# Attention: the turn of a step's maxima moved behind the first three query-major units of the next step

## The reference, cut to what matters

```python
scores = einsum('bnhd,bmd->bhnm', q, k) / sqrt(D)   # causal: keys m <= n alone
attn = softmax(scores, axis=-1)
out = einsum('bhnm,bmd->bnhd', attn, v)
```

## Time and profile before

| | before |
|---|---|
| three runs | 1034.52, 1038.93, 1037.01 us; median 1037.01 |
| the profiled execution | 1033.92 us, span 1032.2 us |
| PE, DVE, ACT, POOL busy, share of the span | 94%, 73%, 56%, 40% |
| mean granted TensorE clock | 0.984 of full speed |
| steady attention steps | from about 125 to 266 us and from 634 to 773 us |

### The profile page before, as it was taken

One profiled execution on the slowest core, in us unless ns is written; L12 is line 12 of the kernel. 1 busy time (PEld: TensorE's weight loads), 2 busy tenths in 40 slices (PEclk: granted clock), 3 DMA queues, 4 the chain that ended last, 5 costly groups with the idle time before them and its releaser, 6 DMA issues.

```text
span 1032.2 us, 19370 instructions
## 1 busy us (share of the span) xinstructions
PE 969.5 (94%) x6562; PEld 625.6 (61%) x6562; DVE 750.2 (73%) x1820; ACT 573.1 (56%) x1078; POOL 409.4 (40%) x434
## 2 busy tenths in 40 slices
PE   4888999999889999999999899999999899999997
PEld 3433333333348889988886433443334588899887
DVE  6788888888346686447868988888882668754475
ACT  4525767777753335653445657777777533466432
POOL 3420635322534507716653202323225361374570
PEclk9969999999999999999999999999999999999999
DMA  4720222110205315644239524333401251266351
GB/s 142 189 50 10 66 44 45 42 41 13 48 9 172 125 46 156 187 114 129 82 93 217 137 41 71 64 64 77 75 14 44 84 174 51 82 192 158 118 183 48
DMA packets 66754, 95.40 MB, mean 92 GB/s; under 512 B 19669, under 2 KB 50821, under 8 KB 64599
## 3 DMA queue, kind: packets, MB, share of 16 engines
q1 hardware_dynamic: 46645, 52.74, 18.9%
q10 hardware_dynamic: 13100, 22.53, 8.7%
q0 software_dynamic: 6912, 18.88, 7.2%
HBM read 66.79 MB, written 26.67 MB: 91 GB/s over the span
## 4 chain that ended last, share of the span: by engine, by line
PE 72%; DVE 13%; DMA 4%; issue 3%; ACT 3%; POOL 2%; SPq 1%; ACTq 0%; DVEq 0%; POOLq 0%
PE o_ps L1092 13%; PE st_ps L1075 10%; PE su_ps L1034 8%; PE st_ps L284 7%; PE st_ps L285 6%; PE st_ps L286 6%; PE st_ps L1034 4%; PE o_ps L1232 3%; PE su_ps L1138 3%; PE su_ps L1232 3%; DVE mab L1716 2%; PE st_ps L1267 2%; DVE unread L1714 2%; DVE xn L1595 1%; PE su_ps L284 1%
## 5 line engine op out<-in xcount | busy, mean ns | idle before, releaser
L1437 ACT ACTIVATE pt<-st_ps 128x512 f32<-128x512 f32 (+1 forms) x584 | 314.7, 596 | 159.5 <-PE st_ps L1075 150.8
L1075 PE MATMUL st_ps<-qs,ks 99*128 99x512 bf16 (+9 forms) x768 | 212.5, 329 | 5.4 <-DMA qs<-nmx 3.3
L798 POOL TENSOR_SCALAR_AFFINE_SELECT pt<-pt 128x512 f32<-128x512 f32 x120 | 74.4, 637 | 315.3 <-ACT pt L1437 315.3
L1034 PE MATMUL su_ps<-ks,qs 102*128 102x512 bf16 (+7 forms) x538 | 160.0, 330 | 7.5 <-DVE mc L1716 2.8
L1092 PE MATMUL o_ps<-pt,vp 128*32 128x512 f32 (+3 forms) x1536 | 155.5, 502 | 0.0
L1716 DVE TENSOR_REDUCE mab<-su_ps 128x1 f32<-128x512 f32 (+2 forms) x211 | 137.6, 684 | 13.0 <-PE su_ps L1034 12.2
L1034 PEld LDWEIGHTS su_ps<-ks,qs 96*128 96x128 bf16 (+1 forms) x538 | 51.7, 98 | 109.2 <-DVE mab L1716 45.5
L879 POOL DMA_INDIRECT rows_in<-rows,source x80 | 78.6, 983 | 98.0 <-DVE source L1975 73.7
L1075 PEld LDWEIGHTS st_ps<-qs,ks 99*128 99x128 bf16 (+2 forms) x768 | 73.4, 99 | 65.3 <-ACT pt L1437 16.9
L1714 DVE CUSTOM_DVE_ANT_0 unread<-su_ps,cst 128x384 f32<-128x384 f32 (+1 forms) x168 | 99.4, 612 | 17.8 <-PE su_ps L1034 17.7
L1463 ACT CAST hh<-hf 128x512 fp32r<-128x512 f32 x64 | 39.7, 621 | 123.9 <-DVE hf L1930 121.7
(11 more groups left out here) (234 smaller groups left out, 2061.3 us busy)
## 6 DMA issues: line engine op xcount, KB each, us to landing
wu_raw<-w_units_dram SPq DMA_DIRECT2D x32, 384.0 KB, 3.2
outs<-rows_out ACTq DMA_DIRECT2D x40, 256.0 KB, 3.2
q_parts<-hml SPq DMA_DIRECT2D x16, 384.0 KB, 3.3
wexp_raw<-w_units_dram SPq DMA_DIRECT2D x16, 384.0 KB, 6.7
inv<-inverses SPq DMA_DIRECT2D x128, 32.0 KB, 1.8
rows<-xn SPq DMA_DIRECT2D x8, 512.0 KB, 6.0
qs<-q_parts ACTq DMA_DIRECT2D x10, 384.0 KB
k_parts<-hml SPq DMA_DIRECT2D x8, 384.0 KB, 2.9
```

What stands on the lines that cost most here:

```text
L798: pool.affine_select(block, block, [[0, 4], [1, P]], ALU.is_ge, 0.0, base=0, channel_multiplier=-1).then_inc(masked, 1)
L1034: last = pe.matmul(out_b[:, c0:c0 + width], query_columns(s, slice(0, rows), j0 + a, P * qt, P * qt + P), key_stack(l, s)(j0 + a)[0:rows, ...
L1075: last = pe.matmul(out_b[:, at:at + hi - lo], key_stack(l, s)(j)[0:rows, P * kt:P * kt + P], query_columns(s, slice(0, rows), j, lo, hi), ...
L1437: act.activation(exponentials(S, q)[:, j, 0:width_of(s, q)], bank[KM_BANKS[i % len(KM_BANKS)]][:, 0:width_of(s, q)], ACT.Exp, scale=1 / np ...
```

## The change

`unit_number` gives the turn of steps 2 to 6 the place in the rotation of banks behind units 0, 1 and 2 of the step after, and those units the numbers before it. In PE's order this turn comes behind unit 2 of the next step; in VectorE's the join stays directly behind unit 37, and the four parts come ahead of unit 3 of the next step. The turns of steps 1 and 7 stay directly behind unit 37. `lead` goes from 0.2 to 0.28, and the reciprocals come ahead of units 9 and 30 in place of 6 and 27.

```diff
+def turned_late(s):
+    return 2 <= s < STEPS - 1
+
+def unit_number(S, u):
+    s = S % STEPS
+    if u == NSU - 1 and turned_late(s):
+        return unit_base(S) + u + UNITS_AHEAD
+    if u < UNITS_AHEAD and turned_late(s - 1):
+        return unit_base(S) + u - 1
+    return unit_base(S) + u
+
+UNITS_AHEAD = 3
...
+    passed = np.cumsum(np.insert(cost[:-1], UNITS_AHEAD, cost[-1])) / cost.sum()
+    passed = np.append(np.delete(passed, UNITS_AHEAD), 1.0)
...
     for s in range(2, STEPS):
-        for u, t in enumerate(s - 1 - lead + through):
+        for u in range(NSU):
+            t = s - 1 - lead + (passed[u] if turned_late(s - 1) else through[u])
             while at[n] < t - 1e-9 or u > 1 and n < FIRST_PIECES - 1:
                 n += 1
-            behind[n].append((s, u))
+            if u < NSU - 1 or not turned_late(s):
+                behind[n].append((s, u))
+            if u == UNITS_AHEAD - 1 and turned_late(s - 1):
+                behind[n].append((s - 1, NSU - 1))
...
-UNITS_BEHIND = [units_behind_pieces(l, 0.2) for l in range(2)]
+UNITS_BEHIND = [units_behind_pieces(l, 0.28) for l in range(2)]
...
-INVERT_AT, DIVIDE_BEHIND = (6, 27), (2, 4)
+INVERT_AT, DIVIDE_BEHIND = (9, 30), (2, 4)
...
+            def join_maxima(l, s):
+                S = step_no(l, s)
+                a = S % 2
+                dve.wait_ge(su_used, unit_base(S) + NSU - 1)
+                dve.tensor_tensor(mc[:, a, :, HALF:QT], mab[:, a, 0, :, :], mab[:, a, 1, :, :], ALU.max).then_inc(mc_done, 1)
...
             def maxima_parts(l, s):
-                n = unit_base(S) + NSU - 1
+                n = unit_number(S, NSU - 1)
                 a = S % 2
-                dve.wait_ge(su_used, n)
-                dve.tensor_tensor(mc[:, a, :, HALF:QT], mab[:, a, 0, :, :], mab[:, a, 1, :, :], ALU.max).then_inc(mc_done, 1)
                 dve.wait_ge(su_ready, n + 1)
...
+                            if u == UNITS_AHEAD and turned_late(s):
+                                maxima_parts(l, s)
                             maximum(l, s + 1, u)
-                        maxima_parts(l, s + 1)
+                        join_maxima(l, s + 1)
+                        if not turned_late(s + 1):
+                            maxima_parts(l, s + 1)
```

More of the change, by code:

```diff
@@ L176, in added_before @@
     if at >= 0:
-        return unit_base(S) + ADDED[at] + 1
-    return unit_base(S - 1) + ADDED[at] + 1 if S else 0
+        return unit_number(S, ADDED[at]) + 1
+    return unit_number(S - 1, ADDED[at]) + 1 if S else 0
 def units_behind_pieces(l, lead):
@@ L1015, in query_major @@
                 qt, half, j0, share, width, _ = SU[u]
-                n = unit_base(step_no(l, s)) + u
+                n = unit_number(step_no(l, s), u)
                 if s and u == 0:
@@ L1702, in maximum @@
                 S = step_no(l, s)
-                n = unit_base(S) + u
+                n = unit_number(S, u)
                 dve.wait_ge(su_ready, n + 1)
```

## The result

The changed kernel takes **1059.88 us** (median of 4 runs, 1059.72 to 1061.7) against 1036.09 us of the kernel before in the same set (4 runs, 1034.52 to 1038.93): a ratio of **1.0229 [1.0212, 1.0246]**. It is slower by 24 us where 13 were forecast, and above the range of 1039 to 1056. The profiled execution has a span of 1058.0 us against 1032.2, 25.8 more, at a mean granted clock of 0.976 against 0.984. Run again beside the second group of experiments it gave 1060.54 us, 1.0223 [1.0197, 1.0250].

The account below looks back on a forecast made before the run. The prediction took attention to be bound by PE's queue, run nearly without a gap. Steps 3 to 6 (+3.8), into step 2 (+1.5) and into step 7 (+1.2) made 6.5 us a layer, +13: 1050 us named, range 1039 to 1056.

Parts of the forecast that it names:

- The parts behind three maxima, and what they meet: VectorE's four parts queue behind three maxima, then GpSimd's products hold them; next first piece 8.4 or 9.5 us, not 7.33.
- The first rival, no hold: GpSimd's products don't stop VectorE's parts, or VectorE gets its turn between them: +4 us, 1041; chance 0.18.
- The faster case: Maxima come in time and PE keeps the gains at the turn, unit 36 and banks: 1029 to 1032 us; chance 0.08.
- the absorbed one: Each step starts later, but PE catches up within the same step: within 3 us of before; chance 0.10.
- the slack: How much later the maxima's DMAs could be issued without delaying the next step's first piece: 0.9 us.
- The recovery of 0.7 a step: PE saves unit 36's issue (0.21), its stall (0.24) and smaller bank waits (0.25 us) within each step.
- Unit 36's two terms: On PE, unit 36's issue of 0.21 us and its stall of 0.24 for a free bank are saved.
- smaller bank waits elsewhere: VectorE starts a step with nothing left over, so PE's other bank waits shrink by 0.25 us, an estimate.
- The step of the two kinds: Steps 3 to 6: +0.4 us where one GpSimd product follows, +1.5 where two follow, two steps of each a layer.
- Into step 2: Eleven units, not eight, behind step 0's last piece (+0.9 us) and a later first piece (+0.6): +1.5 a layer.
- Into step 7: Turn not late but stalls 1.6 us; maxima's DMAs go out 1.9 later, less 0.7 recovered: +1.2 us a layer.
- The upper bound of +20: Whole kernel: every last part held by a second product, and the 0.25 us not recovered ten times: +20 us.

Follow-up runs that it names:

- the kernel kept busy: The changed kernel with six matmuls of 512 columns, later overwritten, run on PE ahead of the first piece's wait in steps 3 and 5: 1090.99 us, 1.0161 of before.

## Why the prediction was right or wrong

The direction and the mechanism of the late parts were right; the size was half of it, because three terms of the sum were wrong or missing.

*The parts behind three maxima, and what they meet* was right to a tenth. The first part was to start 1.91 behind the join and starts 1.89 behind it (214.52 to 216.41); the cast was to be held to 0.5 and takes 0.48; the last part was to take up to 1.5 where a second product follows and takes 1.39, and 0.28 elsewhere; the first piece was to come 3.2 behind the first issue, and with a landing of 1.9 it does. Making the products wait removed both holds (0.21 and 0.28). That a product would hold as a memset and a select did was my estimate from the earlier trace rows; the runs show it: the cast and the last part end 0.07 and 0.14 behind a product's end, and the last part takes 0.28 with GpSimd quiet (608.65). By what mechanism, no run shows. The first rival, no hold, is refuted. Its one piece of evidence, the cast at 211.12 that took 0.21 beside a select, had come too late in the select to show a hold, 0.09 ahead of its end at 211.21: with the lead of 0.32 the cast at 187.23 took 0.33 and ended 0.08 behind its select.

*The faster case and the absorbed one* fell with the slack. Two units fewer would have done: with one ahead, the wait is gone. That would still not have been the faster case, since the turn then stands for 0.88.

*The recovery of 0.7 a step* failed in the part that was an estimate. Unit 36's two terms (0.21 and 0.24) are found at unit 36; the 0.25 of "smaller bank waits elsewhere" is not, and unit 36's 0.24 comes back at other units. Counted from starts, the even step that ends with the turn at 215.44 has, against the one of before that ends at 210.18: bank waits of 0.48 in place of 0.50, the turn's stall 0.45 in place of 0.52, 0.26 ahead of piece 33, where PE waits for an exponential and before did not, and 0.54 at the first piece. That is +0.71 of the +0.73. The step of the two kinds costs +0.73 and +1.81 in place of +0.4 and +1.5, at full clock and with a landing of 1.9. The cleanest measure is the kernel whose products wait: by my terms it should have had 27.94 - 0.7 + 0.73 (its first piece at V+8.06 in place of 7.33) = 27.97 and has 28.40. The last term is off by 0.4 there: about 0.3 a step over the eight late steps, 2.6 us in all.

*A term the sum did not have: the clock.* I asked what PE waits for, and not what PE does after it has waited. From a first piece to the next join it takes 22.18 us at full clock (162.21 to 184.39 in the changed kernel run again, and the same in steps 3 and 5 of the kernel kept busy), and in after 23.54 behind 162.31, 23.54 behind 223.36 and 23.69 behind 743.42: +1.36, +1.36 and +1.5, 4.2 us. That this goes with PE standing is what all twelve traces say together; that it comes of it is inferred. In steps 3 to 6 the clock fell eleven times, each time within 1.5 us of the end of a wait of 1.45 us or more, and never in the kernels without such waits. Behind the waits of 2.7 to 3.2 us in step 5 it fell in seven of eight, and behind the two that were filled with matmuls it did not. Behind waits of 1.45 it fell in two of seven, so in these steps such a wait lay ahead of every fall, but not every such wait had one behind it, and what decides is not known. In step 1 of the second layer it fell with no late first piece ahead (the windows from 620).

A further 2.05 us stands at a low clock behind the second layer's attention. Before has such a stretch there too, a shorter one (3.4 us against 6.9). Nothing was run that ties its length to the change, and it is as short as in before, 3.4 us, in two kernels that keep the late turns (ends as before, reciprocals back); it stays open.

*A second such term: the landing.* In step 5 the third of the maxima's DMAs lands in 3.1 us (first layer) and 3.4 (second), where most take 1.8 to 1.9 (see below), and the wait is 2.71 and 3.00 in place of some 1.45. That is +1.25 and +1.55. In both cases the DMA view shows one packet of the instruction queue, 16 KB, at that time (the line is of the window 221 to 224), and none around step 3 of the first layer:

```profile
q8 instruction: 1, 0.02, 2.0%
```

No run was made to try this, but the twelve traces bear it out. Of the 360 DMAs of the maxima of steps 2 to 6, 20 have such a packet starting within 1.5 us behind their issue, and they land in 2.3 to 3.7 us; 24 have it 1.5 to 1.9 us behind, and land in 1.8 to 2.0; the 293 with no packet of 8 KB or more beside them land in 1.8 to 1.9. In before the packet of step 5 comes at 216.2, when the maxima have landed; in after they go out 2.4 us later behind the join and meet it. Before has a landing of 3.6 us of this kind in step 2 of the first layer, and there the first piece (132.28) does wait for it, 0.98 us. The sum did not use that row (before, the maxima's tile in the window 126.5 to 130), which could have told of the term:

```profile
DMA to landing us min/median/max: 1.8/2.0/3.6
```

*The ends.* Into step 2, +3.0 was said for both layers: steps 1 and 2 together have +0.74 and +3.83. Step 1 varies by 0.9 us between the two traces of the changed kernel (27.21 and 28.09, first layer). The +1.5 of step 1 in the second layer goes with its low clock. It is not tied to the longer burst: that period is 26.1 us in three kernels that have the burst and no such stretch, and 29.8 in the one with the old burst and a stretch. Into step 7, +1.2 a layer was said, and +0.6 and +1.3 found. Giving the ends their old lead gained some 2 us in the median.

The account of the 25.8 us: 13 as forecast; the failed recovery, +2.6; the clock in steps 3 and 5, +4.2; the landings, +2.8; steps 1 and 2, +1.6 (about the low clock in step 1 of the second layer); step 7, -0.5; behind the second attention, +2.05. Sum 25.75.

The failed step, then, is the sum over steps 3 to 6: +3.8 a layer was said, +9.1 and +8.2 were measured. It took every landing as 1.9 where step 5 had 3.1 and 3.4 (2.8 us), priced each wait at its own length and the clock behind it at nothing (4.2 us), and allowed 0.25 a step of recovered bank waits that are not there, beside a turn's stall mis-sized by 0.07 (2.6 us). The upper bound of +20 fell with it, since it was made by adding holds alone.

## What to carry to other kernels

A result moved behind other work is late by everything that its instructions then queue behind, on each engine: here two maxima of 0.61 us used up a slack of 0.9, and the neighbour's two products of 1.3 held what came after. Count that slack first; if it goes, price the wait by its length and by the clock behind it (here 1.36 to 1.5 us where it fell). And to give a consumer distance from its producer, put work between them that makes nothing for the producer's engine: two pieces and a row of values ahead of the turn took its stall away, three units did not.

## What the runs showed of the hardware

- PE's granted clock fell from 1.00 to 0.50 behind single waits in a queue otherwise full: behind 1.46, 2.71 and 3.00 us of standing in after, and 1.77 in the kernel with a lead of 0.32. It did not fall behind 1.45 in after (second layer) and in its second run, nor behind 2.69 in step 2 of the kernel that fills only steps 3 and 5, nor behind 3.16 in the one with the old ends. With the reciprocals back it fell behind a wait of 1.45 (162.25). Length alone does not say which. In after it was back at 1.00 4.5 and 4.9 us behind the end of the wait (windows from 162 and from 223), and 3.7 behind that of 3.00.
- Such a stretch costs 1.35 to 1.5 us of the step, where the windows from 162 to 168 have PE at the lower level for some 3.4 us (twice the missing 0.15, 0.50 and 0.20, times 2 us). Half of that, 1.7, is an estimate of what the lower clock takes; where the rest of it went was not traced.
- With six matmuls that compute nothing in such waits the clock did not fall behind them, and the kernel was not slower but faster: 1.0161 [1.0129, 1.0194] against 1.0229 [1.0212, 1.0246] and 1.0223 [1.0197, 1.0250], measured in different sets.
- A 0.28 us VectorE instruction took 1.39 beside a GpSimd product, a 0.21 one 0.48, while what reads the score banks (st_ps, su_ps) beside the same first product kept its time: the reduction at 215.81 with 0.68, the two parts at 216.41 and 216.71 with 0.27 and 0.28.
- A DMA of 8 KB of the maxima, issued by SyncE, landed in 1.8 to 1.9 us with no instruction-queue packet of 8 KB or more beside it (293 in twelve traces), and in 2.3 to 3.7 us where a 16 KB one started within 1.5 us behind its issue (20). Steps 2 to 6 alone are counted. That the packet is the cause is inferred from this, and no run changed it.
